# Moments first behind conv2, and most Fourier steps between conv1's chunks

## The chip, the cores and the metric

The kernel runs on one core of a Trainium2 chip. The metric is the device time of one execution in microseconds (us). The core has TensorE (PE), VectorE (DVE), ScalarE (ACT), GpSimd (POOL) and SyncE (SP, which here only issues DMAs); the engines run side by side and meet only at semaphores.

## The reference, cut to what matters

```
x = edge_filter(x)                         # prologue: 3x3 conv, softmax, weighted sum of shifts
for j in range(4):                         # 32 channels, 8 images of 64x64
    Kj, Lj = project(K[j]), project(L[j])
    z = relu(batchnorm(conv3x3(x, Kj)))    # conv1, norm 1
    x = x + 0.1 * conv3x3T(z, Kj)          # conv2
    x = batchnorm(x, gamma[j], beta[j])    # moments, norm 2, affine
    t = 1.0 / (0.1 * abs(fft2(Lj)) ** 2 + 1.0)
    x = real(ifft2(fft2(x) * t))
```

The Fourier stage is linear and acts on each channel alone, so the kernel runs it on x before norm 2 is known and applies norm 2's scale and bias to its result (the "affine" step).

## The kernel before, in words

Images go in four pairs (bp 0 to 3). A pair's convolution is four chunks, so conv1 and conv2 have 16 chunks each; a chunk is 12 matmuls into one of 8 PSUM banks (`conv`, L1025). Each layer j is one list, `layer_steps(j)`, and every engine walks that list and does its own part of each step. So a step's place in the list sets its place in five queues at once, each of which is strictly in order.

A pair's Fourier stage is this chain of steps:
- turn: DVE transposes the pair (L923) out of Z0, where POOL has put sums and differences of its halves (`mix_halves`, L474);
- fwdW: PE (L1164), then DVE moves the rows (L933);
- slot0 and fwdH: PE (L1179, L1181, L1193), then DVE multiplies by the layer's table (L957, L968);
- slot0c: PE (L1204), then ACT keeps it (L641); the inverse needs it;
- invH: PE (L1221, in the last layer L1218), then DVE moves (L939);
- invW: PE (L1236), and back: DVE transposes (L950), then POOL adds and subtracts halves (`unmix_halves`, L484);
- affine: ACT scales (L657) in two halves, and SP copies each scaled half, moved by two partition groups, from X0 to X2 (`shift_two`, L389 and L390). conv1 of the next layer reads X0 and X2, so chunks 0, 4, 8 and 12 wait for such copies (`x2_in`).

Norm 2 needs sums over all of x: ACT makes them chunk by chunk (`sum_x`, L635), DVE closes them (moments, L855 to L860), PE averages over partitions (L1139), DVE ends the norm (to L880). `prepare` (L707, four instructions) makes the weights of conv1 and of the next conv2 out of the next layer's parameters; `sum_kernels` (L697) comes ahead of it. `prepare_taps` (L719 to L731) starts the next layer's table, behind conv1's chunk 6. On DVE conv1's statistics are L810, and conv2's result is added to x by L908. ACT copies conv1's result out of PSUM (L550).

A step that takes a bank waits until the bank's last use is drained. `number_banks` gives banks in the list's order, so a new order also changes who waits for whom. fwdW and invW take four banks at once.

## Time and profile before

| | us |
|---|---|
| median of 3 runs (698.69 to 700.88) | 698.69 |
| the profiled execution | 700.2 |
| its span | 698.4 |
| PE busy in the span | 619.7 |
| DVE busy | 493.7 |
| ACT busy | 343.7 |
| POOL busy | 233.3 |

The profile is of one execution; 1.8 us of its time lie outside the span. Layers 0, 1 and 2 start conv2 at 179.73, 316.39 and 453.19 and repeat each other nearly to the 0.1 us, so what is read in one holds for three. Layer 1's conv2 runs from 316.4 to 379.5, layer 2's conv1 from 395.4 to 447.0. The last layer starts conv2 at 591.48 and has no conv1 behind it.

### The profile page before, as it was taken

The numbers are of one execution on the slowest core, as the hardware profiler recorded it, in microseconds if no ns is written. First come the engines' busy times: TensorE is split into PE (matmuls) and PEld (weight loads), VectorE is DVE, ScalarE is ACT, GpSimd is POOL, SyncE is SP. The second block draws the span as 40 slices with busy tenths as digits, with TensorE's granted clock in tenths as the row PEclk, the third lists the DMA queues.
The fourth block names the chain that finished last, engine by engine and source line by source line (L and its number), as shares of the span: only waits on it lengthen the run. The fifth ranks groups of instructions, "written<-read, shape, count | busy, mean of one in ns | idle before, by whom it ended". The sixth has DMA issues, their size and how long they took to land.

```text
span 698.4 us, 14578 instructions
## 1 busy us (share of the span) xinstructions
PE 619.7 (89%) x5840; PEld 200.9 (29%) x5840; DVE 493.7 (71%) x875; ACT 343.7 (49%) x640; POOL 233.3 (33%) x180
## 2 busy tenths in 40 slices
PE   6498999999999979999898899998978989989783
PEld 4122333222332223233232222332222223323221
DVE  2679888865786785738868767486778554867674
ACT  1466666652894322419932314299223233982232
POOL 0367666771142432202225222022252220222200
PEclk9699999999999999999999999999999999999988
DMA  9995111117600022294000224930004159000044
GB/s 187 182 168 97 32 32 33 31 31 161 157 1 1 1 63 62 70 224 116 1 2 1 70 55 107 224 79 1 2 1 109 30 133 218 3 2 1 1 123 120
DMA packets 44786, 51.21 MB, mean 73 GB/s; under 512 B 36528, under 2 KB 36656, under 8 KB 42672
## 3 DMA queue, kind: packets, MB, share of 16 engines
q1 hardware_dynamic: 40240, 48.99, 32.8%
q10 hardware_dynamic: 4480, 1.30, 1.2%
q8 instruction: 47, 0.77, 0.5%
q14 instruction: 19, 0.16, 0.1%
HBM read 11.99 MB, written 4.19 MB: 23 GB/s over the span
## 4 chain that ended last, share of the span: by engine, by line
PE 54%; ACT 20%; DVE 14%; issue 6%; DMA 3%; SPq 1%; POOL 0%; DVEq 0%; ACTq 0%; POOLq 0%
PE psum L1025 29%; ACT Z L613 10%; PE psum L1097 6%; ACT work L635 6%; PE psum L1164 3%; PE psum L1048 3%; DVE Z L950 2%; DMA X<-X 2%; PE psum L1221 2%; PE psum L1193 2%; PE psum L1236 2%; DVE work L923 2%; PE psum L1085 2%; DVE work L968 2%; DVE work L933 1%
## 5 line engine op out<-in xcount | busy, mean ns | idle before, releaser
L1025 PE MATMUL psum<-X,wts 128*32 128x512 f32 x1536 | 171.3, 594 | 9.1 <-DMA X<-X 5.0
L1025 PE MATMUL psum<-Z,wts 128*32 128x512 f32 x1536 | 172.3, 594 | 4.3 <-DVE Z L890 4.3
L474 POOL TENSOR_TENSOR Z<-X 128x512 f32<-128x512 f32 x64 | 80.8, 1286 | 251.2 <-DVE X L908 251.2
L635 ACT ACTIVATE work<-X,small 128x512 bf16<-128x512 f32 x128 | 90.7, 710 | 87.7 <-DVE X L908 87.7
L550 ACT ACTIVATE Z<-psum 128x512 f32<-128x512 f32 x64 | 38.2, 596 | 140.4 <-PE psum L1025 129.3
L484 POOL TENSOR_TENSOR X<-Z 128x1024 f32<-128x1024 f32 x24 | 56.9, 2394 | 113.0 <-DVE Z L950 113.0
L810 DVE BATCH_NORM_STATS2 stats<-Z 128x6 f32<-128x512 f32 x60 | 41.0, 691 | 69.7 <-ACT Z L550 69.6
L1025 PEld LDWEIGHTS psum<-Z,wts 128*32 128x32 f32 x1536 | 50.1, 109 | 115.5 <-issue 106.9
L613 ACT ACTIVATE Z<-Z,small 128x512 f32<-128x512 f32 (+4 forms) x92 | 80.3, 922 | 5.2 <-DVE small L880 4.7
L1025 PEld LDWEIGHTS psum<-X,wts 128*32 128x32 f32 x1536 | 47.8, 109 | 121.4 <-issue 109.8
L908 DVE SCALAR_TENSOR_TENSOR X<-psum,X 128x512 f32<-128x512 f32 x64 | 44.2, 690 | 36.2 <-PE psum L1025 36.0
L933 DVE STREAM_TRANSPOSE work<-psum 128x512 f32<-128x512 f32 x64 | 40.0, 698 | 18.3 <-PE psum L1164 18.3
L950 DVE STREAM_TRANSPOSE Z<-psum 128x512 f32<-128x512 f32 x64 | 39.9, 681 | 8.0 <-PE psum L1236 8.0
L799 DVE TENSOR_TENSOR work<-Z,psum 128x512 f32<-128x512 f32 x52 | 33.6, 680 | 16.9 <-PE psum L1085 16.9
L968 DVE TENSOR_TENSOR work<-psum,tabT 128x496 f32<-128x496 f32 x64 | 38.6, 665 | 5.8 <-PE psum L1193 5.8
L1164 PE MATMUL psum<-work,cstS 32*64 32x512 f32 x384 | 33.1, 639 | 8.9 <-DVE Z L950 4.9
L1097 PE MATMUL psum<-work,cstS 128*32 128x512 f32 x168 | 36.9, 631 | 2.9 <-DVE spare L799 2.7
L799 DVE TENSOR_TENSOR spare<-Z,psum 128x512 f32<-128x512 f32 x48 | 30.9, 679 | 4.8 <-PE psum L1085 4.6
L464 POOL TENSOR_TENSOR tabT<-Z,work 128x512 f32<-128x512 f32 x21 | 24.9, 1197 | 25.0 <-PE psum L1097 25.0
L534 ACT ACTIVATE work<-psum 128x512 f32<-128x512 f32 x53 | 30.6, 594 | 3.6 <-PE psum L1085 1.0
L923 DVE STREAM_TRANSPOSE work<-Z 128x512 f32<-128x512 f32 x48 | 31.0, 705 | 0.0
L1193 PE MATMUL psum<-work,cstS 64*64 64x496 f32 x256 | 30.3, 589 | 0.0
(127 smaller groups left out, 819.5 us busy)
## 6 DMA issues: line engine op xcount, KB each, us to landing
...
```

The source lines that it names most:

```text
L474: nc.gpsimd.tensor_tensor(rows(Z0, REG, bp, CH * (2 * half + i), CH), low, high, op=op)\
L484: nc.gpsimd.tensor_tensor(dst, even, odd, op=op).then_inc(parts_added, 1)
L613: last = nc.scalar.activation(z, z, ACT.Relu, bias=small[p0:p1, 13:14], scale=small[p0:p1, 12:13])
L635: nc.scalar.activation(by_row(rest[:, o:o + N // 2].bitcast(bf16)), xc, what, bias=small[:, 26:27], accum_out=sums[:, NCH * i + c:NCH * i ...
L799: nc.vector.tensor_tensor(by_line(product(c, dj, r)), around(c, dj, r), by_line(bank(n)), op=ALU.mult)\
L923: last = nc.vector.transpose(dst[:, b], src.rearrange("p g (e l b) -> p b g e l", e=2, b=2)[:, b])
L933: nc.vector.transpose(freqw[:, N * q:N * q + N], src).then_inc(rows_moved, 1)
L950: last = nc.vector.transpose(dst, src)
L968: nc.vector.tensor_tensor(to, src, tt, op=ALU.mult).then_inc(drained[n % BANKS], 1)
L1025: last = nc.tensor.matmul(out_b[C * r:C * r + C, :], weights[:, o:o + C], rows(src, reg, bp, g, CH, dj - 1), start=(dj == 0), stop=(dj == ...
L1097: last = nc.tensor.matmul(bank(n)[C * r:C * r + C, :], cm(C_STACK, C), product(c, dj, r), start=(dj == 0), stop=(dj == 2), tile_position=( ...
L1164: last = nc.tensor.matmul(bank(first + r)[64 * half:64 * half + 64, :], cstS[k, C_FW + 64 * hi:C_FW + 64 * hi + 64], src[:, hi], start=(hi ...
```

## The change

Layers 0 to 2, behind conv2 (the last layer has a list of its own, `last_steps`, close to the old order):
- Pair 1's invH goes ahead of conv2's chunk 14 and pair 2's fwdW behind it (before: the other way round, each one chunk earlier or later).
- slot0c of pairs 0 and 1 goes behind the next conv2 chunk. A new step, "scaled", says where DVE multiplies by the table; before, that was at the PE steps.
- Behind conv2 stand half of pair 2's fwdH, its slot0 and pair 1's invW, then moments and norm 2, and then the other half of fwdH. On DVE back of pair 1, the second half of the multiplication and turn of pair 3 stand behind the norm.
- Pair 2's slot0c and invH and pair 3's fwdW move from ahead of conv1's chunk 0 to behind chunks 0, 2 and 3. The steps after them move back too: pair 2's invW from behind chunk 2 to behind 4, pair 3's fwdH from 1 to 5, its invH from 3 to 6, its invW from 5 to 7.
- `prepare` is cut in two: conv1's half behind conv2's chunk 13, the other at its old place.
- `mix_halves` of the last chunk waits for norm 2, and ACT's sums are spread over conv2's chunks by a table, SUMS.

```diff
@@ layer_steps
-        9: fourier(j, 1, "fwdW"),
+        9: [("slot0c", j, 0)] + fourier(j, 1, "fwdW"),
-        13: fourier(j, 2, "fwdW"),
-        14: fourier(j, 1, "invH"),
-        15: fourier(j, 2, "fwdH"),
+        13: fourier(j, 1, "invH"),
+        14: fourier(j, 2, "fwdW"),
-    steps += [("moments", j), ("norm", j, 2), ("affine", j, 0), ("turn", j, BP - 1), ("weights", j)]
-    steps += fourier(j, 1, "invW") + [("back", j, 1)] + fourier(j, 3, "fwdW") + fourier(j, 2, "invH")
+    steps += quarters("fwdH", j, 2, (0, 1)) + [("slot0", j, 2), ("scaled", j, 2, 0)] + fourier(j, 1, "invW")
+    steps += [("moments", j), ("norm", j, 2)] + quarters("fwdH", j, 2, (2, 3))
+    steps += [("affine", j, 0), ("back", j, 1, 0), ("back", j, 1, 1)]
+    steps += [("scaled", j, 2, 1), ("turn", j, BP - 1), ("weights", j)]
...
+        6: [("slot0c", j, 3)] + fourier(j, 3, "invH"),
+        7: fourier(j, 3, "invW") + [("back", j, 3, 0), ("back", j, 3, 1)],
@@ mix_halves (POOL)
+                if bp == BP - 1 and i == 1 and j + 1 < DEPTH:
+                    pool.wait_ge(bn_ready, 2 * j + 2)
@@ DVE, "weights" and conv2's chunk 13
-                        prepare()
+                        prepare((1,))
...
                             sum_kernels(j + 1)
+                            prepare((0,))
@@ forward_h (PE)
+                if q == 0:
+                    pe.wait_ge(rows_moved, Q * (BP * j + c // Q + 1))
```

What this does to the queues, at three places. First DVE in layer 0, from back of pair 0 over conv2's chunks 13 to 15; before:

```order
L950 STREAM_TRANSPOSE Z<-psum 128x2x8x32 x4
L908 SCALAR_TENSOR_TENSOR X<-psum,X 128x4x128
L697 TENSOR_REDUCE ksum<-parS 128x64
L933 STREAM_TRANSPOSE work<-psum 128x512 x4
L908 SCALAR_TENSOR_TENSOR X<-psum,X 128x4x128
L939 STREAM_TRANSPOSE spare<-psum 128x8x2x32 x4
L908 SCALAR_TENSOR_TENSOR X<-psum,X 128x4x128
L957 TENSOR_TENSOR work<-psum,tabT 128x64
L968 TENSOR_TENSOR work<-psum,tabT 128x16x31 x4
L855 TENSOR_REDUCE small<-sums 128x2
```

and the same place now (in this file L968 is back, L926 conv2's sum, L725 `prepare`, L957 and L951 the moves of invH and fwdW, L986 the multiplication, L873 the first of moments):

```order
L968 STREAM_TRANSPOSE Z<-psum 128x2x8x32 x4
L926 SCALAR_TENSOR_TENSOR X<-psum,X 128x4x128
L715 TENSOR_REDUCE ksum<-parS 128x64
L725 SCALAR_TENSOR_TENSOR wts<-ksum,cstS,parS 128x96 x2
L957 STREAM_TRANSPOSE spare<-psum 128x8x2x32 x4
L926 SCALAR_TENSOR_TENSOR X<-psum,X 128x4x128
L951 STREAM_TRANSPOSE work<-psum 128x512 x4
L926 SCALAR_TENSOR_TENSOR X<-psum,X 128x4x128
L986 TENSOR_TENSOR work<-psum,tabT 128x16x31 x2
L975 TENSOR_TENSOR work<-psum,tabT 128x64
L873 TENSOR_REDUCE small<-sums 128x2
```

Two of the weights' instructions now stand between chunk 13's sum and the moves, and two multiplications instead of four ahead of the moments. Second PE in layer 0, from conv2's chunk 15 to conv1's first chunks; before:

```order
L1025 MATMUL psum<-Z,wts 32x512 x12
L1179 MATMUL psum<-work,cstS 128x2x16
L1181 MATMUL psum<-work,cstS 64x2x16 x2
L1193 MATMUL psum<-work,cstS 64x496 x8
L1204 MATMUL psum<-work,cstS 64x2x16 x4
L1139 MATMUL psum<-small,cstS 128x5
L1236 MATMUL psum<-spare,cstS 32x512 x16
L1164 MATMUL psum<-work,cstS 64x512 x16
L1221 MATMUL psum<-work,cstS 64x512 x8
L1025 MATMUL psum<-X,wts 32x512 x24
```

and now (L1047 is a convolution, L1219 fwdH, L1262 invW, L1161 the average, L1230 slot0c, L1247 invH, L1188 fwdW):

```order
L1047 MATMUL psum<-Z,wts 32x512 x12
L1219 MATMUL psum<-work,cstS 64x496 x4
L1203 MATMUL psum<-work,cstS 128x2x16
L1205 MATMUL psum<-work,cstS 64x2x16 x2
L1262 MATMUL psum<-spare,cstS 32x512 x16
L1161 MATMUL psum<-small,cstS 128x5
L1219 MATMUL psum<-work,cstS 64x496 x4
L1047 MATMUL psum<-X,wts 32x512 x12
L1230 MATMUL psum<-work,cstS 64x2x16 x4
L1047 MATMUL psum<-X,wts 32x512 x24
L1247 MATMUL psum<-work,cstS 64x512 x8
L1047 MATMUL psum<-X,wts 32x512 x12
```

invW now stands ahead of the average, and nothing but half of fwdH stands between the average and conv1. Third DVE in layer 0 behind conv1's chunk 4; before:

```order
L810 BN_STATS stats<-Z 128x6 x2
L950 STREAM_TRANSPOSE Z<-psum 128x2x8x32 x4
L810 BN_STATS stats<-Z 128x6
L719 TENSOR_REDUCE lsum<-parS 128x32
L721 SCALAR_TENSOR_TENSOR lsum<-lsum,parS 128x96
L724 TENSOR_SCALAR lsum<-lsum,cstS 128x32
L725 SCALAR_TENSOR_TENSOR lsum<-lsum,cstS 128x32
L728 TENSOR_TENSOR work<-lsum,cstS 128x1024
L731 TENSOR_TENSOR work<-work,lsum 128x1024
L810 BN_STATS stats<-Z 128x6 x8
```

and now (L828 is the statistics, L737 to L749 `prepare_taps`, L957 invH's move, L968 back):

```order
L828 BN_STATS stats<-Z 128x6
L737 TENSOR_REDUCE lsum<-parS 128x32
L739 SCALAR_TENSOR_TENSOR lsum<-lsum,parS 128x96
L742 TENSOR_SCALAR lsum<-lsum,cstS 128x32
L743 SCALAR_TENSOR_TENSOR lsum<-lsum,cstS 128x32
L746 TENSOR_TENSOR work<-lsum,cstS 128x1024
L749 TENSOR_TENSOR work<-work,lsum 128x1024
L957 STREAM_TRANSPOSE spare<-psum 128x8x2x32 x4
L828 BN_STATS stats<-Z 128x6
L968 STREAM_TRANSPOSE Z<-psum 128x2x8x32 x4
L828 BN_STATS stats<-Z 128x6 x7
```

`prepare_taps` kept its place behind chunk 6, and pair 3's invH move and back, which stood ahead of it, now stand behind it.

## Rows read from the trace of the kernel before

**Rows 1.** Page, part 5: ACT's copies, count, busy us and mean ns, idle.
```profile
L550 ACT ACTIVATE Z<-psum 128x512 f32<-128x512 f32 x64 | 38.2, 596 | 140.4 <-PE psum L1025 129.3
```

**Rows 2.** Timeline: start us, us, engine, instruction [idle before <-releaser]; layer 1's conv2.
```profile
336.47 5.36 PE L1025 MATMUL psum<-Z,wts 128*32 128x512 f32 x48
...
349.88 0.66 PE L1164 MATMUL psum<-third,cstS 32*64 32x512 f32 x4 [1.50 <-ACT work L641]
...
370.29 0.66 PE L1164 MATMUL psum<-work,cstS 32*64 32x512 f32 x4 [1.22 <-DVE Z L950]
```

**Rows 3.** Timeline, DVE and POOL behind conv2's chunk 13 in layer 1.
```profile
370.11 4.74 POOL L484 TENSOR_TENSOR X<-Z 128x1024 f32<-128x1024 f32 x2 [7.58 <-DVE Z L950]
...
370.53 1.19 DVE L697 TENSOR_REDUCE ksum<-parS 128x64 f32<-128x576 f32 x1
...
376.03 2.51 DVE L939 STREAM_TRANSPOSE spare<-psum 128x512 f32<-128x512 f32 x4 [0.29 <-PE psum L1221]
...
379.63 0.69 DVE L908 SCALAR_TENSOR_TENSOR X<-psum,X 128x512 f32<-128x512 f32 x1 [1.09 <-PE psum L1025]
```

**Rows 4.** Timeline from moments to conv1's first chunk, layer 1.
```profile
383.51 0.18 DVE L855 TENSOR_REDUCE small<-sums 128x2 f32<-128x32 f32 x1
...
384.75 0.36 PE L1139 MATMUL psum<-small,cstS 128*128 128x5 f32 x2 [2.58 <-DVE small L860]
...
385.19 3.61 PE L1236 MATMUL psum<-spare,cstS 64*32 64x512 f32 x32
...
387.15 2.38 ACT L657 ACTIVATE X<-X,small 128x1024 f32<-128x1024 f32 x2 [1.23 <-DVE small L880]
...
389.39 0.97 DVE L707 SCALAR_TENSOR_TENSOR wts<-ksum,cstS,parS 128x96 f32<-128x96 f32 x4
...
389.53 1.98 PE L1164 MATMUL psum<-work,cstS 32*64 32x512 f32 x32 [0.73 <-DVE work L923]
...
395.39 5.36 PE L1025 MATMUL psum<-X,wts 128*32 128x512 f32 x48 [1.35 <-DVE work L933]
...
410.60 1.95 PE L1221 MATMUL psum<-work,cstS 64*64 64x512 f32 x16
```

**Rows 5.** Windows: stretch, us, PE, PEld, DVE, ACT, POOL busy, PEclk, DMA, GB/s.
```profile
386.00:387.00 1.00, 1.00 (x24) 0.38 (x16) 0.86 (x6) 0.00 (x0) 0.00 (x0) 0.50 0.00 0
...
665.00:672.00 7.00, 5.13 (x49) 1.10 (x34) 5.39 (x11) 4.81 (x4) 0.00 (x0) 0.51 0.41 105
```

**Rows 6.** Timeline, DVE in the prologue, beside POOL and without it.
```profile
58.56 2.00 DVE L707 SCALAR_TENSOR_TENSOR wts<-ksum,cstS,parS 128x96 f32<-128x96 f32 x4
...
58.80 1.19 POOL L464 TENSOR_TENSOR X<-Z,work 128x512 f32<-128x512 f32 x1
...
58.88 1.23 DVE L707 SCALAR_TENSOR_TENSOR wts<-ksum,cstS,parS 128x96 f32<-128x96 f32 x1
...
159.82 0.24 DVE L724 TENSOR_SCALAR lsum<-lsum,cstS 128x32 f32<-128x32 f32 x1
```

**Rows 7.** Timeline, conv1's second half in layer 1; last row layer 2.
```profile
419.64 15.67 PE L1025 MATMUL psum<-X,wts 128*32 128x512 f32 x144
...
422.46 4.77 POOL L484 TENSOR_TENSOR X<-Z 128x1024 f32<-128x1024 f32 x2 [7.02 <-DVE Z L950]
...
423.13 0.69 DVE L810 BATCH_NORM_STATS2 stats<-Z 128x6 f32<-128x512 f32 x1 [0.74 <-ACT Z L550]
...
425.02 2.26 DVE L724 TENSOR_SCALAR lsum<-lsum,cstS 128x32 f32<-128x32 f32 x1
...
428.74 1.23 DVE L731 TENSOR_TENSOR work<-work,lsum 128x1024 f32<-128x1024 f32 x1
...
430.71 2.36 ACT L657 ACTIVATE X<-X,small 128x1024 f32<-128x1024 f32 x2
...
436.52 10.51 PE L1025 MATMUL psum<-X,wts 128*32 128x512 f32 x96 [1.22 <-DMA X<-X]
...
574.82 10.51 PE L1025 MATMUL psum<-X,wts 128*32 128x512 f32 x96 [2.67 <-DMA X<-X]
```

More of the change, by code:

```diff
@@ L156, in layer_steps, with last_steps @@
     for c in range(NCH):
[L157 to L160 removed]
+        steps += [("conv1", j + 1, c)] + rest.get(c, [])
+    return steps
+def last_steps(j):
+    steps = fourier(j, 2, "fwdH") + [("slot0c", j, 2), ("moments", j), ("norm", j, 2), ("affine", j, 0), ("turn", j, BP - 1)]
+    steps += fourier(j, 1, "invW") + [("back", j, 1, 0), ("back", j, 1, 1)] + fourier(j, 3, "fwdW") + fourier(j, 2, "invH")
+    steps += [("affine", j, 1)] + fourier(j, 3, "fwdH") + [("slot0c", j, 3)] + fourier(j, 2, "invW")
+    steps += [("back", j, 2, 0), ("back", j, 2, 1)] + fourier(j, 3, "invH") + fourier(j, 3, "invW")
+    return steps + [("back", j, 3, 0), ("back", j, 3, 1), ("affine", j, 2), ("affine", j, 3)]
+SUMS = {c: (c,) for c in range(5)} | {6: (5,), 8: (6,), 9: (7,), 10: (8,), 11: (9, 10), 12: (11,), 13: (12, 13), 14: (14,), 15: (15,)}
 ORDER = prologue_order()
```

53 lines of the change are left out of this document (29 added, 24 removed).

## The prediction, made before the change was run

> **What bounds the kernel now.** I read first the busy times by engine, then the timeline of PE with the idle time ahead of each group, then, at each pause, what released it. PE is busy for 619.7 of 698.4 us and the others far less, so time can come only from PE's pauses, from work at a low clock, or go into new pauses. In layer 1's conv2 PE pauses for ACT and DVE, 1.50 us at most [rows 2]. Behind conv2 the large pause stands: 2.58 us ahead of the average, then invW at 3.61 us, which takes 1.95 elsewhere, and short pauses up to conv1 at 395.39 [rows 4]. In that stretch the granted clock is 0.50, 1.2 instead of 2.4 GHz [rows 5]. So such a drop costs 3.61 - 1.95 = 1.66 us. Behind that PE runs nearly without a pause to chunk 12, which waits 1.22 us for the copy of the last scaled image [rows 7]. Layers 0, 1 and 2 are alike, so a layer's sum counts three times.
>
> I walk through layer 1 with its own times: conv chunk 2.7 us, 2.6 in a run (15.67 for six) [rows 7]; fwdW, invH, invW 1.9 each [rows 4]; fwdH 1.7, slot0 0.6, slot0c 0.3; a DVE move of four 2.5 [rows 3]; an ACT copy 0.6 [rows 1].
>
> **conv2, part by part.** Up to chunk 8 nothing moves; it ends at 341.8. slot0 and fwdH end at 344.1, chunk 9 at 346.8, and slot0c no longer waits. fwdW of pair 1 needs chunk 9 added by DVE, 348.15, where it started at 349.88 before [rows 2]. ACT's sums are not late for it, since SUMS leaves one out. Chunk 11 ends at 357.4, fwdH at 359.7, chunk 12 at 362.4; invW of pair 0 waits until chunk 12 is drained, 363.4, and chunk 13 ends at 368.0 against 369.0 before. Back ends at 368.1, and POOL starts unmix at once, for 4.74 us [rows 3], so to 372.9. DVE adds chunk 13 (to 368.8), sums the kernels (1.19, to 370.0) and comes to the two new instructions of `prepare` in the middle of unmix.
>
> Here is the **price of the cut `prepare`**. Alone, four take 0.97 us [rows 4]. Beside POOL they took 2.00: the first ended with one POOL instruction, and the second lasted 1.23, to the end of the next, which began at 58.80 [rows 6]. L724 shows the same: 0.24 without POOL [rows 6], 2.26 beside unmix, to unmix's end [rows 7]. Unmix is two instructions of about 2.37, so the first of the two gets through at 370.5 and the second at 372.9: DVE goes on at 373.1 and not at 370.5. The bounds are 0.5 us (both get through between POOL's two) and 3.1; I take 3.1, by the nearest row, the second L707. Behind DVE stands invH's move (373.1 to 375.6), and fwdW of pair 2 needs three quarters of it, so PE, which has ended chunk 14 at 372.6, pauses 2.5 us to 375.1. Chunk 15 ends at 379.7 and is added at 379.9, where it was 379.63 [rows 3]. So of 2.2 us that the new order wins in conv2, nothing is left. And a pause of 2.5 us is next to the one of 2.58: I take the drop of the clock for it too, **+1.66**; its bounds are 0 and 1.66.
>
> **From conv2 to conv1.** Before, from chunk 15's addition to affine 387.15 - 379.63 = 7.52 us. Now DVE multiplies only two quarters and slot0 ahead of moments, but fwdH starts later, behind the row moves; moments start 2.6 us behind the addition and not 3.9, so affine follows it by 6.3. PE's invW (1.9) fits in ahead of the average. From affine to conv1 before 8.24, since conv1 waited for DVE's move of fwdW's rows. Now it waits for the copy alone: from ACT's start to a conv1 chunk released by the copy 436.52 - 430.71 = 5.8 [rows 7]. So conv1 starts at 379.9 + 6.3 + 5.8 = 391.9 and not at 395.39: **-3.5**. But PE has ended the second half of fwdH at about 385.5 and stands still for some 6 us, longer than the pause in rows 4, so the first chunks of conv1 run at the low clock: **+1.65** (bounds 0.8 and 2.6, since rows 5 show a stretch of 7 us at 0.51).
>
> **Moved into conv1.** What filled the wait before has its price now: slot0c 0.3, invH 1.9, fwdW 1.9: **+4.1**. The copy for chunk 4 is asked for behind chunk 2's copy on ACT, and PE does invH, chunk 3 and fwdW meanwhile, 6.5 us against 0.6 + 5.8: no margin, no price. invW of pair 2 waits for the moves of fwdW, which DVE starts 2.3 us behind fwdW's start: **+0.3**.
>
> **Behind chunk 6** three queues meet. ACT's affine 2 waits for POOL's unmix, whose last half ends about when chunk 6 does; then 1.24 for the second half, 0.6 for chunk 6's copy, slot0c's copy 0.3, and invH of pair 3 needs that: 1.9 us of pause. DVE: statistics 0.7 behind the copy, then `prepare_taps`, which takes from the end of chunk 6's statistics at 423.8 to 430.0, 6.2 us [rows 7], of which 2.0 are L724's wait for POOL; unmix is over by then, so 4.2; then invH's move, 2.5. invW of pair 3 needs that. From chunk 6's end 0.1 + 1.75 + 0.7 + 4.2 + 2.5 + 0.1 = 9.3 us. PE has slot0c, invH and chunk 7 in that time, 4.9: **+4.4**. Behind it back, unmix and affine 3 lie as before, and affine 3 still stands behind chunk 9's copy, so chunk 12's wait stays.
>
> **The sum.** A layer: -3.5 + 1.66 + 1.65 + 4.1 + 0.3 + 4.4 = +8.6; three layers +25.8. The last layer has no `prepare` and no unmix; it keeps the win in conv2, about 2.0 of the 2.2, and its tail is in the old order: -2.0. Together +23.8, so the profiled execution's 700.2 would be 724.0. Its own time is 1.5 above the median; on the median the sum gives 698.69 + 23.8 = 722.5.
>
> **A rule weighed.** Rows 4 and 5 show that a pause of 2.58 us was followed by the low clock, all four times. The Trainium skill, page "TensorE: Matmul & The Clock Gate", section "Why this matters for your kernels", warns only of pauses longer than this one. By it the pause ahead of fwdW costs nothing but itself, and the sum is 5.0 lower.
>
> **Rivals.**
> - No drop for the 2.5 us pause: 25.8 - 5.0 - 2.0, 717.5. For it: the pause of 1.50 us led to none [rows 2]; against it, the four of 2.58. The skill's rule above speaks for it.
> - The two `prepare` instructions slip between POOL's two: then the conv2 win stays, per layer -2.6 of stall and no drop ahead of fwdW, 8.6 - 4.3 = 4.3; 698.69 + 13.0 - 2.0 = 709.7. Against it: both rows of rows 6.
> - More drops: invW of pair 3 waits some 2.5 us as well, and the low stretch at conv1's start can be the long one. +1.66 and +0.9 a layer: 730.
> - Faster: the pauses behind chunk 6 are covered. That needs ACT, DVE's taps and the move to fit in the 4.9 us that PE has from chunk 6 to invW 3, and `prepare` not to stall. Then -6.1 (the early start without the stall) + 4.1 + 0.3 + 1.65 = 0.0 a layer, and with the -2.0 of the last layer 696.6; with no drop at conv1's start 691.7. It decides at 4.9 us: 4.2 + 2.5 alone are more, so it needs DVE to do these steps in another order than its queue has.
> - The change starts conv1 early only on paper: the copy lands later than 5.8, as in layer 2, where chunk 12 waited 2.67 and not 1.22 [rows 7]. +1.45 a layer, 726.9.
>
> **Chances.** Forecast with all its terms (719 to 726) 0.35; no drop for the short pause 0.2; `prepare` slipping through, with or without parts of the rest (705 to 715), 0.17; more drops or late copies (over 726) 0.17; the faster rival 0.07; little changed 0.04. The range 706 to 730 leaves out the faster rival, the unchanged case and the end of the slow ones. Three tenths of a per cent, 2 us, is what a measurement of this kernel can tell from no change: faster 0.07, within 0.05, slower 0.88.
>
> **What would show it.** Behind conv2's chunk 13 one of two DVE weight instructions lasting over 2 us and a PE pause of about 2.5 us ahead of fwdW; conv1 starting about 3.5 us (2 with the drop) earlier relative to conv2's start than now, out of a PE pause of 6 us, with PEclk at 0.5 there; pauses of about 1.9 and 2.5 us ahead of pair 3's invH and invW, the latter released by the move; chunk 12 still waiting about 1.2 us; conv2 starts 8.6 us further apart than the 136.8 us of now. I would be wrong above all if DVE got through beside unmix, or if `prepare_taps` took well under 4.2 us.

## The result, and the profile after

The changed kernel takes 723.04 us (median of 4 runs, 718.95 to 724.63), the kernel before 699.4 (4 runs on the same chip, 698.69 to 700.88): a ratio of 1.033, with a 95% interval of 1.028 to 1.037. Slower, as forecast; the prediction was 722.5 in a range of 706 to 730. The profiled run took 723.0, its span is 721.1.

The page of after, the head and part 1, the granted clock of part 2, and the groups of part 5 that changed:

```profile
span 721.1 us, 14584 instructions
...
PE 627.7 (87%) x5840; PEld 200.6 (28%) x5840; DVE 498.1 (69%) x875; ACT 344.0 (48%) x640; POOL 233.0 (32%) x180
...
PEclk9699999999999879999999899999998999999988
...
L1047 PE MATMUL psum<-X,wts 128*32 128x512 f32 x1536 | 180.3, 615 | 25.2 <-issue 20.3
L1047 PE MATMUL psum<-Z,wts 128*32 128x512 f32 x1536 | 172.4, 594 | 4.3 <-DVE Z L908 4.3
```

PE's instructions are the same 5840. Its busy time is 8.0 us more (619.7 before) and its idle time 14.7 us more. Of the 8.0 some 5 are low clock (an estimate: what the slow groups of both timelines take over their usual length); the rest I put down to the moved steps, which break conv1's chunks into shorter runs. Conv1's convolutions take 180.3 us against 172.4 for conv2's, which have the same count and shapes, and the idle time ahead of them is 25.2 us, 20.3 of it ahead of chunk 0.

To see where the time went I cut each layer at three starts in PE's timeline: stretch A from conv2's chunk 0 to conv1's chunk 0, B from there to conv1's chunk 12, C from there to the next conv2. The last layer has no conv1 and is one stretch, up to the end of the span. All in us:

| kernel | A, layers 0, 1, 2 | B, layers 0, 1, 2 | C, layers 0, 1, 2 | last layer | from conv2 of layer 0 to the end |
|---|---|---|---|---|---|
| before | 79.0, 79.0, 79.0 | 41.0, 41.1, 42.6 | 16.7, 16.7, 16.7 | 106.9 | 518.7 |
| after | 77.1, 75.4, 75.4 | 54.3, 51.3, 52.8 | 16.7, 16.7, 18.4 | 105.0 | 542.9 |
| difference | -1.9, -3.6, -3.6 | +13.3, +10.2, +10.2 | 0, 0, +1.7 | -1.9 | +24.2 |
| forecast | -1.8 each | +10.5 each | 0 | -2.0 | +23.8 |

What lies ahead of layer 0's conv2 is the same work in both, and takes 178.1 to 183.8 us over the kernels of this study without a pattern; so I compare the last column, and give the medians beside it. That column is of one execution each, and the runs of the kernel before alone, over all chips, lie between 697.6 and 706.4 us: differences of a few us in it say little by themselves, and the stretches in which they arise say more.

After's PE timeline in layer 1, where conv2 starts 9.83 us later than before's (columns as in [rows 2]):

```profile
326.22 18.25 PE L1047 MATMUL psum<-Z,wts 128*32 128x512 f32 x168 [1.07 <-DVE Z L908]
...
385.04 0.66 PE L1188 MATMUL psum<-work,cstS 32*64 32x512 f32 x4 [2.28 <-DVE spare L957]
...
393.51 0.36 PE L1161 MATMUL psum<-small,cstS 128*128 128x5 f32 x2
...
401.60 4.05 PE L1047 MATMUL psum<-X,wts 128*32 128x512 f32 x24 [6.75 <-issue]
...
432.48 1.95 PE L1247 MATMUL psum<-work,cstS 64*64 64x512 f32 x16 [1.41 <-ACT work L658]
...
439.36 1.09 PE L1262 MATMUL psum<-spare,cstS 64*32 64x512 f32 x16 [2.22 <-DVE spare L957]
...
452.88 10.51 PE L1047 MATMUL psum<-X,wts 128*32 128x512 f32 x96 [1.12 <-DMA X<-X]
```

The pause of 2.58 us ahead of the average [rows 4] is gone. A pause of 2.28 us ahead of fwdW has come, one of 6.75 ahead of conv1's chunk 0, with 4.05 us for a chunk of 2.78 behind it, and pauses of 1.41 and 2.22 ahead of pair 3's invH and invW. Chunk 12 waits 1.12 us, where it was 1.22 [rows 7]. DVE and POOL where the pause ahead of fwdW comes from, to be read against [rows 3]:

```profile
378.19 4.76 POOL L501 TENSOR_TENSOR X<-Z 128x1024 f32<-128x1024 f32 x2 [7.54 <-DVE Z L968]
...
380.07 2.99 DVE L725 SCALAR_TENSOR_TENSOR wts<-ksum,cstS,parS 128x96 f32<-128x96 f32 x2
382.99 2.50 DVE L957 STREAM_TRANSPOSE spare<-psum 128x512 f32<-128x512 f32 x4
```

Two small instructions of `prepare` take 2.99 us and end when POOL's unmix does. In the code they wait for no semaphore of POOL, so that the engines meet only at semaphores, as the description of the chip says above, does not hold for DVE and POOL here. Behind chunk 6 ACT and DVE show where the other two pauses come from:

```profile
428.08 1.25 ACT L674 ACTIVATE X<-X,small 128x1024 f32<-128x1024 f32 x1 [1.83 <-POOL X L501]
430.44 1.24 ACT L674 ACTIVATE X<-X,small 128x1024 f32<-128x1024 f32 x1 [1.11 <-POOL X L501]
...
432.07 0.27 ACT L658 ACTIVATE work<-psum 128x64 f32<-128x64 f32 x1
...
432.81 0.43 DVE L737 TENSOR_REDUCE lsum<-parS 128x32 f32<-128x288 f32 x1
...
433.57 0.24 DVE L742 TENSOR_SCALAR lsum<-lsum,cstS 128x32 f32<-128x32 f32 x1
...
436.54 2.51 DVE L957 STREAM_TRANSPOSE spare<-psum 128x512 f32<-128x512 f32 x4
```

ACT waits for each half of unmix (1.83, 1.11), and only then copies the chunk and slot0c. DVE's tap weights run from 432.81 to 436.5, and the move for invW stands behind them.

### The profile page after: what moved, and what is told of

It is laid out like the page before. It is cut to its first block, busy times and chain, and to the rows that moved or that the text cites. A ratio compares the mean times of both kernels' runs of the same rounds, so it can differ in the third digit from the quotient of the medians.

```text
span 721.1 us, 14584 instructions
## 1 busy us (share of the span) xinstructions
PE 627.7 (87%) x5840; PEld 200.6 (28%) x5840; DVE 498.1 (69%) x875; ACT 344.0 (48%) x640; POOL 233.0 (32%) x180
## 4 chain that ended last, share of the span: by engine, by line
PE 56%; DVE 18%; issue 14%; POOL 5%; ACT 3%; DMA 3%; SPq 1%; DVEq 0%; ACTq 0%; POOLq 0%
PE psum L1047 31%; PE psum L1119 6%; PE psum L1188 4%; POOL X L501 4%; PE psum L1262 3%; DMA X<-X 2%; PE psum L1070 2%; DVE spare L957 2%; DVE work L986 2%; DVE work L951 2%; PE psum L1107 2%; PE psum L1219 2%; DVE X L926 1%; DVE wts L725 1%; ACT X L674 1%
## 5 line engine op out<-in xcount | busy, mean ns | idle before, releaser
L1047 PE MATMUL psum<-X,wts 128*32 128x512 f32 x1536 | 180.3, 615 | 25.2 <-issue 20.3
L1047 PE MATMUL psum<-Z,wts 128*32 128x512 f32 x1536 | 172.4, 594 | 4.3 <-DVE Z L908 4.3
L652 ACT ACTIVATE work<-X,small 128x512 bf16<-128x512 f32 x128 | 90.7, 710 | 76.7 <-DVE X L926 76.3
L828 DVE BATCH_NORM_STATS2 stats<-Z 128x6 f32<-128x512 f32 x60 | 41.4, 690 | 89.0 <-ACT Z L567 89.0
L1047 PEld LDWEIGHTS psum<-X,wts 128*32 128x32 f32 x1536 | 47.2, 112 | 146.2 <-issue 133.9
L1047 PEld LDWEIGHTS psum<-Z,wts 128*32 128x32 f32 x1536 | 50.3, 109 | 121.9 <-issue 113.7
L630 ACT ACTIVATE Z<-Z,small 128x512 f32<-128x512 f32 (+4 forms) x92 | 80.3, 922 | 5.2 <-DVE small L898 4.7
L926 DVE SCALAR_TENSOR_TENSOR X<-psum,X 128x512 f32<-128x512 f32 x64 | 43.5, 680 | 29.0 <-PE psum L1047 28.4
L951 DVE STREAM_TRANSPOSE work<-psum 128x512 f32<-128x512 f32 x64 | 39.9, 685 | 20.6 <-PE psum L1188 20.6
L968 DVE STREAM_TRANSPOSE Z<-psum 128x512 f32<-128x512 f32 x64 | 40.1, 684 | 14.3 <-PE psum L1262 14.2
L986 DVE TENSOR_TENSOR work<-psum,tabT 128x496 f32<-128x496 f32 x64 | 38.8, 664 | 5.5 <-PE psum L1219 5.2
L1188 PE MATMUL psum<-work,cstS 32*64 32x512 f32 x384 | 34.6, 656 | 8.2 <-DVE spare L957 6.8
L674 ACT ACTIVATE X<-X,small 128x1024 f32<-128x1024 f32 x24 | 29.1, 1237 | 13.6 <-POOL X L501 9.8
L1219 PE MATMUL psum<-work,cstS 64*64 64x496 f32 x256 | 31.0, 591 | 0.5 <-DVE work L951 0.2
```

Source lines behind the costliest of these rows:

```text
L630: last = nc.scalar.activation(z, z, ACT.Relu, bias=small[p0:p1, 13:14], scale=small[p0:p1, 12:13])
L652: nc.scalar.activation(by_row(rest[:, o:o + N // 2].bitcast(bf16)), xc, what, bias=small[:, 26:27], accum_out=sums[:, NCH * i + c:NCH * i ...
L926: nc.vector.scalar_tensor_tensor(xc, in0=by_row(bank(n)), scalar=STEP, in1=xc, op0=ALU.mult, op1=ALU.add).then_inc(drained[n % BANKS], 1)
L951: nc.vector.transpose(freqw[:, N * q:N * q + N], src).then_inc(rows_moved, 1)
L986: nc.vector.tensor_tensor(to, src, tt, op=ALU.mult).then_inc(drained[n % BANKS], 1)
L1047: last = nc.tensor.matmul(out_b[C * r:C * r + C, :], weights[:, o:o + C], rows(src, reg, bp, g, CH, dj - 1), start=(dj == 0), stop=(dj == ...
```

## The experiments

The theory is the sum of the prediction: two stalls on DVE (`prepare` beside POOL, the tap weights ahead of the move), one on ACT (affine 2 ahead of slot0c), a pause of PE ahead of conv1 with a low clock behind it, and 4.1 us of work moved into conv1. The main rival from the result: the low clock, and not the stalls, is what costs, and comes back somewhere else when a stall is taken out. Three runs of the changed kernel take out one of these each; two more take out several. The others try the change's order inside conv2 without the rest, what the low clock costs, and what delays a copy. The table has all of them, in the columns of the table above; the ratios are those to the kernel before of the same chip, with their 95% intervals:

| kernel | A | B | C | last layer | to the end | median, ratio |
|---|---|---|---|---|---|---|
| `prepare` behind chunk 12 | 73.0, 73.1, 73.0 | 51.2, 54.0, 55.4 | 16.7, 16.7, 18.4 | 103.3 | 534.7 | 718.11, 1.022 (1.016 to 1.027) |
| taps behind chunk 8 | 75.4, 75.4, 75.4 | 50.4, 49.4, 51.7 | 16.7 each | 103.6 | 531.3 | 714.09, 1.016 (1.012 to 1.020) |
| PE kept busy | 76.9, 75.3, 75.3 | 51.6, 51.6, 51.5 | 16.7 each | 103.3 | 535.6 | 716.96, 1.021 (1.017 to 1.025) |
| both cures | 73.0, 73.1, 73.1 | 50.1, 50.1, 51.6 | 16.7 each | 103.6 | 524.5 | 707.61, 1.011 (1.007 to 1.016) |
| no stalls | 73.1, 73.0, 73.0 | 46.8, 46.8, 46.8 | 16.7 each | 105.8 | 515.3 | 696.27, 0.994 (0.991 to 0.997) |
| new conv2 alone | 78.0, 77.3, 77.2 | 41.0, 41.1, 42.4 | 16.7 each | 103.4 | 510.4 | 694.94, 0.988 (0.983 to 0.993) |
| banks | 76.5, 76.7, 77.2 | 41.0, 40.9, 43.2 | 16.7, 16.7, 18.1 | 103.6 | 510.5 | 692.00, 0.987 (0.983 to 0.991) |
| invW first | 80.0, 79.6, 79.9 | 41.3, 40.9, 43.7 | 16.7, 16.7, 18.0 | 103.6 | 520.3 | 700.53, 1.001 (0.998 to 1.003) |
| before, kept busy | 79.8, 79.8, 80.3 | 41.0, 41.0, 41.0 | 16.7 each | 106.1 | 519.0 | 700.28, 0.999 (0.996 to 1.001) |
| banks, kept busy | 78.4, 78.4, 78.5 | 41.5, 41.5, 41.4 | 16.7 each | 105.8 | 515.4 | 696.29, 0.993 (0.990 to 0.996) |
| new conv2, shifted | 77.9, 77.3, 77.2 | 41.0, 41.0, 41.0 | 16.7 each | 105.0 | 510.4 | 693.33, 0.989 (0.984 to 0.993) |
| banks, shifted | 77.0, 76.6, 77.3 | 42.0, 41.0, 41.7 | 16.7 each | 103.4 | 509.0 | 688.41, 0.982 (0.977 to 0.986) |

**`prepare` behind chunk 12**, where POOL has nothing to do:

```diff
-                        elif at[1] == 13 and j + 1 < DEPTH:
+                        elif at[1] == 12 and j + 1 < DEPTH:
                             sum_kernels(j + 1)
                             prepare((0,))
```

> The changed kernel with the sum of the kernels and conv1's half of prepare one chunk earlier, behind conv2's chunk 12, where POOL stands still until back is done. My theory (the two weight instructions wait for POOL's unmix): the second one takes 0.25 us instead of about 2.8, the pause of 2.27 us ahead of pair 2's fwdW goes, conv1 starts some 2.5 us earlier after conv2's start in layers 0 to 2, total 7 to 10 us below the changed kernel (the upper end if drops of the clock go with it). Rival (the pause ahead of fwdW is the move of invH, wherever prepare stands, or the time is given back in front of moments): within 2 us of the changed kernel.

Its timeline in layer 1: DVE's `prepare` and the first fwdW of pair 2 on PE, then conv1's chunk 0 and pair 3's invW.

```profile
368.85 0.55 DVE L725 SCALAR_TENSOR_TENSOR wts<-ksum,cstS,parS 128x96 f32<-128x96 f32 x2
...
377.21 0.66 PE L1188 MATMUL psum<-work,cstS 32*64 32x512 f32 x4
...
393.81 5.31 PE L1047 MATMUL psum<-X,wts 128*32 128x512 f32 x24 [6.77 <-issue]
...
432.82 3.50 PE L1262 MATMUL psum<-spare,cstS 64*32 64x512 f32 x32 [2.22 <-DVE spare L957]
```

The two instructions take 0.55 us and fwdW has no pause. Stretch A is 73.0 us in all three layers, 2.35 less than after's layers 1 and 2, and 4.0 less than layer 0, which had the low clock there too. So the stall was worth 2.35 us a layer. (The edit also moves the sum of the kernels, 1.2 us, out of the way; but the two instructions alone became 2.44 us shorter, more than the pause.) In all, 8.2 us less than the changed kernel, within the 7 to 10 expected. B is longer by 2.7 and 2.6 us in layers 1 and 2 for another reason: chunk 0 takes 5.31 and not 4.05, and invW of pair 3 3.50 and not 1.95. On that point the rival is right: the low clock came in other places, and took part of the gain.

**The taps behind chunk 8**, where PE has a run of chunks ahead of it that needs nothing from DVE:

```diff
-                        if at[1] == 6:
+                        if at[1] == 8:
```

> The changed kernel with prepare_taps behind conv1's chunk 8 instead of 6, so behind pair 3's invH move and back on DVE, and now beside POOL's unmix of pair 3. My theory: the pause of 2.2 us ahead of pair 3's invW goes; that of 1.4 us ahead of invH stays, since it is ACT's; total 6 to 9 us below the changed kernel. Rival (chunk 12 waits for affine 3 anyway, so what is won there is waited for later): chunk 12's wait grows from 1.1 to 3.3 us and the total stays within 2 us.

PE at the same place in layer 1, pair 3's invH, chunk 7 and invW, and DVE's L742 of the moved taps:

```profile
431.19 1.95 PE L1247 MATMUL psum<-work,cstS 64*64 64x512 f32 x16 [1.42 <-ACT work L658]
...
435.78 1.95 PE L1262 MATMUL psum<-spare,cstS 64*32 64x512 f32 x32
...
443.02 2.26 DVE L742 TENSOR_SCALAR lsum<-lsum,cstS 128x32 f32<-128x32 f32 x1
```

invW follows chunk 7 at once. L742, beside POOL's unmix again, takes 2.26 us and not 0.24, and nobody waits for it. So the same instruction is long beside unmix and short without it, as those of `prepare` are. Chunk 12 waits no longer than before in layers 0 and 1 (1.01 and 1.10), so the rival is out. The gain is 11.6 us, more than the 6 to 9 expected: 6.7 are the pause (2.23 in each layer); most of the rest is where the low clock fell: not at fwdW in layer 0 (A -1.7), not at invW in layer 0 (-1.3), not in layer 2's C (-1.7) and not in the last layer (-1.4), but more at chunk 0 in layers 1 and 2 (+0.4, +1.3).

**PE kept busy ahead of conv1**: six matmuls ahead of each of the three conv1, into the bank that chunk 0 overwrites.

```diff
+                if c == 0 and j:
+                    bk.claim(NUMBER["conv1", j, c])
+                    for _ in range(6):
+                        nc.tensor.matmul(bank(NUMBER["conv1", j, c]), cm(C_AVG), cstS[:, 0:N], start=True, stop=True)
```

> The changed kernel with six matmuls of 128 by 512 added in PE's 6.8 us pause ahead of conv1's chunk 0 in layers 1 to 3, into the bank that chunk 0 then overwrites; they are beside the computation. My theory (conv1's start pays for a low clock): PEclk stays 1.00, chunk 0 takes 2.8 us instead of 4.05 and 5.35, total 4 to 7 us below the changed kernel. Rival (chunk 0 is slow from the copies that land beside it, or the clock falls all the same): chunk 0 keeps over 4 us, total within 2 us or higher.

PE's timeline in layer 1, the added matmuls (each in two records), conv1's chunk 0, and pair 3's invW:

```profile
395.97 5.42 PE L1060 MATMUL psum<-cstS 128*128 128x512 f32 x12
402.75 2.78 PE L1047 MATMUL psum<-X,wts 128*32 128x512 f32 x24 [1.36 <-DMA X<-X]
...
439.23 3.49 PE L1266 MATMUL psum<-spare,cstS 64*32 64x512 f32 x32 [2.22 <-DVE spare L957]
```

The pause of 6.75 becomes 5.42 us of work and one of 1.36, released by the copy; chunk 0 takes 2.78 in all three layers and starts when it did. So the low clock behind the long pause cost 1.3 to 2.6 us a layer, as much as chunk 0 was over 2.78, 5.1 in all. In all three layers invW of pair 3 now ran slow, 3.24 to 3.61 us behind a pause of 2.22, where after had it in one: 3.2 of the 5.1 us went there. Most of the total gain of 7.3 us (4 to 7 expected) is therefore not the theory's: layer 2's chunk 12 waited 0.99 us and not 2.60 and ran at full clock behind it, 3.3 us together, and the last layer, which the edit doesn't touch, was 1.7 shorter.

**Both cures together:**

> The changed kernel with both cures at once: the first half of prepare behind conv2's chunk 12 instead of 13, and the tap weights behind conv1's chunk 8 instead of 6. Alone, from conv2's start in layer 0 to the end of the span, the first took 8.2 us off the changed kernel's 542.9 and the second 11.6. If the two stalls are what they seem, two pauses far apart with nothing shared, the gains add: 542.9 - 19.8 = 523.1 from conv2's start on, and about 1.006 times the kernel before (518.7 + 4.4). The rival: part of each gain was the low clock, and this comes back at another pause when one is removed (invW of pair 3 ran at 3.5 us in two layers of the first cure). Then the second cure, which removes that very pause, should bring more than its own share, 521 or less; and if instead the drops are only moved on to conv1's start and chunk 12, less than the sum, 526 or more.

524.5 us from conv2's start, 1.4 over the sum of the two, and between the two numbers by which the expectation would know the rival. A has the first one's 73.0 and B the second one's lack of a pause. The stalls are apart, and their gains add, as near as the low clock lets one see: chunk 0 of conv1 takes 5.2 to 5.4 us in all three layers, in after 4.1 in two of them.

**No stalls**: both cures, the matmuls ahead of conv1, and ACT's affine 2 behind chunk 6's slot0c:

```diff
-        5: fourier(j, 3, "fwdH") + [("affine", j, 2)],
-        6: [("slot0c", j, 3)] + fourier(j, 3, "invH"),
+        5: fourier(j, 3, "fwdH"),
+        6: [("slot0c", j, 3), ("affine", j, 2)] + fourier(j, 3, "invH"),
```

> Both cures, and on top: affine of quarter 2 stands behind chunk 6's slot0c instead of behind chunk 5, so ACT's slot0c copy does not queue behind it (pause of 1.41 us ahead of invH of pair 3), and six 128x512 matmuls whose result is overwritten run in the pause ahead of conv1's chunk 0 in layers 1 and 2 and the first. By my sum what is then left of the change is the moved work (+4.1 a layer), conv1 started earlier by 3.5 + 2.6 = 6.1, invW of pair 2 +0.3, and no low clock at conv1's start: -1.7 a layer, and -2.0 in the last layer: 518.7 - 5.1 - 2.0 = 511.6 from conv2's start on, ratio about 0.99. The rival, that the moved work costs more than its own busy time in conv1 (copies for chunks 4 and 12 come late, affine 2 now delays its own chunk), gives 518 to 521 and a ratio of 1.00 or over.

PE's timeline in layer 1: conv1's chunk 0, invW of pair 2, invH of pair 3:

```profile
387.64 2.78 PE L1047 MATMUL psum<-X,wts 128*32 128x512 f32 x24 [1.36 <-DMA X<-X]
...
405.69 1.95 PE L1266 MATMUL psum<-work,cstS 64*32 64x512 f32 x32 [0.42 <-DVE work L951]
...
416.46 1.95 PE L1251 MATMUL psum<-work,cstS 64*64 64x512 f32 x16 [0.63 <-ACT work L658]
```

All three layers are alike to 0.1 us. A is 6.0 us shorter than before's, where the sum had 6.1. B is 5.7 longer than before's layer 1: 4.2 are the moved work (slot0c 0.35, invH 1.9, fwdW 1.9), 0.42 and 0.63 are pauses ahead of invW and invH, and the rest, 0.5, I take for the gaps between more and shorter runs of chunks, since a chunk that stands alone takes 2.7 us and one in a run 2.6. So without its stalls the change is worth -0.1 and -0.3 us in layers 0 and 1, and not my -1.7, because pauses and gaps around the moved work cost 1.5 where I had 0.3. In layer 2 it is -1.8, since before's chunk 12 waits 1.6 us longer there, which is no merit of the order (see "Shifted"). The last layer has 105.8, 0.8 more than after's, with invW and fwdW at the low clock. My expectation was 3.7 too low, and the rival's 2.7 too high.

**The new conv2 alone**: the change's order inside conv2, and all that stands behind it as before.

```diff
-    steps += quarters("fwdH", j, 2, (0, 1)) + [("slot0", j, 2), ("scaled", j, 2, 0)] + fourier(j, 1, "invW")
-    steps += [("moments", j), ("norm", j, 2)] + quarters("fwdH", j, 2, (2, 3))
-    steps += [("affine", j, 0), ("back", j, 1, 0), ("back", j, 1, 1)]
+    steps += fourier(j, 2, "fwdH") + [("slot0c", j, 2), ("moments", j), ("norm", j, 2), ("affine", j, 0)]
...
-                        prepare((1,))
+                        prepare((0, 1))
...
-                            prepare((0,))
```

> One part of the change alone: the new order inside conv2 (slot0c one chunk later, pair 1's invH ahead of pair 2's fwdW, the spread sums), and behind conv2 the old order, with all of prepare at its old place and no wait on POOL. My theory: 2.0 to 2.2 us less in each of four layers, since the new order is only spoilt by prepare's stall: 690 to 692 us, faster than the kernel before by over 1%. Rival (the order in conv2 is worth something only in the last layer, where no unmix and no sum of kernels stand on DVE): 696 to 699 us.

510.4 us, 8.3 less than before: A -1.0, -1.7 and -1.8, and -3.5 in the last layer, where fwdW takes 1.98 us and in before 3.72. The expectation had 2.0 to 2.2 in each of four layers: its total (8.0 to 8.8) came by luck, since the three layers gave less and the clock in the last one made up for it. This part of the change is good for about 1.2% (0.988, against the kernel before on the same chip), and the rest of it, with its `prepare` and its steps in conv1, costs 32.5 us on top.

One more thing stands in its timeline of layer 1, from the average to conv1:

```profile
386.73 1.95 PE L1254 MATMUL psum<-spare,cstS 64*32 64x512 f32 x32 [0.24 <-issue]
...
388.54 2.38 ACT L669 ACTIVATE X<-X,small 128x1024 f32<-128x1024 f32 x2 [1.23 <-DVE small L893]
...
390.92 2.98 PE L1180 MATMUL psum<-work,cstS 32*64 32x512 f32 x32 [2.23 <-DVE work L936]
...
394.16 2.50 DVE L946 STREAM_TRANSPOSE work<-psum 128x512 f32<-128x512 f32 x4
...
396.80 5.36 PE L1041 MATMUL psum<-X,wts 128*32 128x512 f32 x48 [0.39 <-DVE work L946]
```

Here invW ran at 1.95 us behind a pause of 2.57 and not at 3.61 [rows 4], and yet conv1 starts 396.80 - 388.54 = 8.26 us behind affine, where it was 8.24. The prediction had taken 1.66 us as what such a drop costs. (fwdW ran slow here in its place, 2.98 us, so this row alone doesn't settle it.)

**Before, kept busy** asks for that directly:

```diff
+                for _ in range(4 if which == 2 else 0):
+                    nc.tensor.matmul(bank(n), cm(C_AVG), cstS[:, 0:N], start=True, stop=True)
                 pe.wait_ge(moments_in, 2 * j + which)
```

> The kernel before with one addition: ahead of the average behind conv2 PE runs four 128x512 fp32 matmuls whose result is overwritten, so that its pause of 2.58 us becomes one of under 1 us. It asks what the low clock behind that pause costs, 3.61 us for invW instead of 1.95, which the prediction took as 1.66 us. First theory, from the two runs just taken: in the run with the new conv2 alone, layer 1 ran this invW at 1.95 us, and yet conv1 started 8.26 us behind affine, where the kernel before needs 8.24; DVE runs without a gap from the average to its move of the rows that conv1's bank waits for, so PE's slow invW costs nothing there. invW then takes 1.95 in all layers, conv1 starts as before, and the time stays within 2 us of the kernel before, ratio 1.00. The rival: the drop costs 1.66 in each of four layers and the time falls by 5 to 7 us, ratio 0.991.

PE's timeline in layer 1: the four matmuls, the average, invW, fwdW, conv1:

```profile
383.21 3.70 PE L1139 MATMUL psum<-cstS 128*128 128x512 f32 x8
386.75 0.28 PE L1141 MATMUL psum<-small,cstS 128*128 128x5 f32 x2
386.96 1.95 PE L1238 MATMUL psum<-spare,cstS 64*32 64x512 f32 x32
391.45 2.47 PE L1166 MATMUL psum<-work,cstS 32*64 32x512 f32 x32 [2.54 <-DVE work L923]
...
397.31 4.93 PE L1025 MATMUL psum<-X,wts 128*32 128x512 f32 x44 [0.36 <-DVE work L933]
```

The four took 3.70 us, more than the pause, so the average comes 0.9 us later than before (386.75 - 317.50 against 384.75 - 316.39), and conv1 0.8 later. invW takes 1.95 in all four layers. If its slow run had cost 1.66 us, conv1 would have started 0.8 earlier; it didn't, and not in layer 0 either (A 79.8), where fwdW took 1.98 as well. So in layers 0 to 2 the drop there costs next to nothing: PE waits for DVE behind it, 2.54 us now where it was 0.73. The 1.66 us are what invW loses, not what the kernel loses. The total says less than A does, since it hides two other things: chunk 12 of layer 2 waits 1.07 us and not 2.67, and the last layer is 0.8 us shorter although its average comes 0.9 later. There fwdW took 1.98 us and not 3.72, so in the last layer, which has no conv1, the low clock did cost.

**Banks**: the kernel with the new conv2, with invH of pair 2 ahead of fwdW of pair 3, and with conv1's half of `prepare` behind conv2's chunk 12. (The expectation speaks of chunks 12 and 14; in the kernel that ran the other half of `prepare` stays at its old place, behind the norm.)

```diff
-    ... + fourier(j, 3, "fwdW") + fourier(j, 2, "invH")
+    ... + fourier(j, 2, "invH") + fourier(j, 3, "fwdW")
...
-                        prepare((0, 1))
+                        prepare((1,))
...
-                        elif at[1] == 13 and j + 1 < DEPTH:
+                        elif at[1] == 12 and j + 1 < DEPTH:
                             sum_kernels(j + 1)
+                            prepare((0,))
```

> The kernel before's order behind conv2 with the changed kernel's order inside conv2 (as in the run with the new conv2 alone, which took 510.4 us from conv2's start on), and two more edits: invH of pair 2 ahead of fwdW of pair 3, so that the bank that conv1's chunk 0 takes is not the one whose rows DVE has to move last, and prepare split over chunks 12 and 14 of conv2. The first says that the wait before conv1 (1.35 us in the kernel before, released by DVE) is a matter of the bank and not of the copy: conv1 then starts 1.3 us earlier in each of three layers, and the split brings up to 0.5 more: 505 to 506 us, ratio about 0.98. The rival: the copy of the first scaled image lands no earlier than that, and the pause only changes its releaser: 509 to 511.

In the total 510.5 us, as with conv2 alone. A is 1.5 and 0.6 us shorter than with conv2 alone in layers 0 and 1, and the same in layer 2. The pause only changed its place: chunk 0 follows fwdW at once, and fwdW waits 1.85 to 3.62 us for DVE's move of back. PE's timeline, fwdW and conv1 in layer 1, and fwdW in layer 2:

```profile
390.86 1.98 PE L1183 MATMUL psum<-work,cstS 32*64 32x512 f32 x32 [2.43 <-DVE Z L963]
392.77 5.36 PE L1042 MATMUL psum<-X,wts 128*32 128x512 f32 x48
...
524.91 2.71 PE L1183 MATMUL psum<-work,cstS 32*64 32x512 f32 x32 [3.62 <-DVE Z L963]
```

The rival holds for the total (510.5), though not its reason. The releaser is DVE's back (L963), and not the copy; fwdW's own input was turned 3.2 us before it starts, so I read the wait as one for the banks that back frees, late in DVE's queue.

**invW first**, ahead of the moments:

```diff
-    steps += fourier(j, 2, "fwdH") + [("slot0c", j, 2), ("moments", j), ("norm", j, 2), ("affine", j, 0)]
+    steps += fourier(j, 2, "fwdH") + [("slot0c", j, 2)] + fourier(j, 1, "invW") + [("moments", j), ("norm", j, 2), ("affine", j, 0)]
...
-    steps += fourier(j, 1, "invW") + [("back", j, 1, 0), ("back", j, 1, 1)] + ...
+    steps += [("back", j, 1, 0), ("back", j, 1, 1)] + ...
```

> As the run on banks, with invW of pair 1 taken out from behind the turn and put behind slot0c, ahead of the average, where PE pauses for 2.58 us in the kernel before and then runs invW at 3.61 us instead of 1.95. If filling the pause keeps the clock up, PE saves invW's extra 1.66 us and starts conv1 up to that much earlier: 500 to 502 us from conv2's start on, ratio 0.97. The rival: DVE, not PE, sets the pace there (its moments stand behind the row moves, and conv1 waits for the copy), so that PE only waits longer ahead of conv1, and the pause there, longer now, puts the clock down at conv1's chunk 0: no gain against the run on banks, or 1 us a layer lost.

PE's timeline in layer 1: invW of pair 1, the second half of invH, fwdW:

```profile
384.06 1.95 PE L1257 MATMUL psum<-spare,cstS 64*32 64x512 f32 x32 [0.58 <-issue]
...
392.60 1.99 PE L1242 MATMUL psum<-work,cstS 64*64 64x512 f32 x8 [5.17 <-issue]
395.64 3.42 PE L1183 MATMUL psum<-work,cstS 32*64 32x512 f32 x32 [1.05 <-DVE work L952]
```

The pause of 2.58 is filled, and one of 5.17 stands in the middle of invH. 520.3 us, 9.8 more than banks and worse than the rival expected. invH's second half starts while DVE's move of back runs; I read that as the bank which this move frees, which wasn't tested. fwdW behind it takes 3.42 us and conv1 needs it.

**Banks, kept busy**, with the four 128x512 matmuls ahead of the average:

> The run on banks (510.5 us from conv2's start in layer 0 to the end of the span) with the same four matmuls ahead of the average. In that run layers 0 and 1 took 134.1 and 134.3 us, 1.2 less than with the new conv2 alone, but layer 2 took 138.6: fwdW at 2.71 us behind a pause of 3.62, chunk 12 to 15 at 11.98 instead of 10.51 behind a pause of 2.44. Theory: DVE sets the pace from the average to conv1, and the drops behind other pauses fall where they will, so these matmuls change little: invW at 1.95, layers between 134 and 138, 508 to 512. The rival: PE kept busy there holds the clock up for all that comes behind it up to conv1, fwdW takes 1.98 in every layer, and layer 2 comes to 136 or less: 505 to 507.

515.4 us, more than either theory had. The matmuls delay the average by 0.9 us, as in before, and fwdW, now behind a pause of 3.78 us, takes 3.11 to 3.17 us in each of the three layers, where banks had 1.98, 1.98 and 2.71. Here work ahead of one pause did not keep the clock up behind the next.

**Shifted.** Layer 2's chunk 12 waits 2.67 us in before and 1.22 in layer 1 [rows 7]. I looked for what else moves in that copy. Queues of the DMA engines in half a microsecond of before, 571.0 to 571.5, and in the run below, 565.0 to 565.5:

```profile
q8 instruction: 1, 0.02, 14.3%
```

```profile
q8 instruction: 1, 0.02, 10.9%
```

SyncE's issues and PE's chunk 12 of before, layer 2:

```profile
568.81 0.46 SPq L389 DMA_DIRECT2D X<-X  x1
...
574.82 1.50 PE L1025 MATMUL psum<-X,wts 128*32 128x512 f32 x12 [2.67 <-DMA X<-X]
```

One packet of the queue named `instruction`, 0.02 MB, moves while the copy is under way (issued from 568.81 on). Before and after and the twelve experiments have 42 such copies ahead of a chunk 12. In eight of them, all in layer 2, this packet starts 3.0 to 3.4 us ahead of chunk 12, and the wait is 2.4 to 2.8 us; in the other 34 it starts 4.3 us or more ahead, and the wait is 0.9 to 1.2. (The expectation below has these distances by half microseconds and a little too large.) Four matmuls of 128x8 in the pause ahead of the average shift the place of that packet:

```diff
+                for _ in range(4 if which == 2 else 0):
+                    nc.tensor.matmul(bank(n)[:, 0:8], cm(C_AVG), cstS[:, 0:8], start=True, stop=True)
```

> The run with the new conv2 alone, plus four very small fp32 matmuls of 128x8 ahead of the average in PE's pause there, whose result is overwritten: they cost no time that anyone waits for, but shift where in the program each load of instructions falls. It asks why chunk 12 of conv1 waits 2.4 to 2.7 us for its copy in layer 2 of eight kernels (this one: 2.46) and about 1.0 in layers 0 and 1. In each of these eight an instruction packet of 0.02 MB moves 3.3 to 3.6 us ahead of chunk 12, while the copy runs; in the kernels with added matmuls it moves 6.5 us or more ahead, and the wait is 1.0 to 1.1. Theory: the packet delays the copy. With the shift it falls ahead of the copy in layer 2, the wait is 1.1 there, and that layer is 1.4 us shorter than 136.3: 509 from conv2's start on, instead of 510.4. The rival: the wait belongs to layer 2 for another reason (the copy's own address or the 6 us of kept clock in those kernels), then it stays at 2.4 to 2.7. If the packet lands in the copy of another layer, that layer should show the long wait instead.

The same two rows of its timeline, layer 2:

```profile
566.95 0.46 SPq L401 DMA_DIRECT2D X<-X  x1
...
571.38 10.51 PE L1041 MATMUL psum<-X,wts 128*32 128x512 f32 x96 [1.09 <-DMA X<-X]
```

The packet now moves at 565.0, ahead of the copy's issue, and chunk 12 starts 4.4 us behind the first issue, with a wait of 1.09; with the new conv2 alone these are 5.8 and 2.46. SyncE issues the four parts at the same distances in both, so it is the copy that is later and not its issue. Layer 2 is 134.9 us and not 136.3, as expected. The total stays at 510.4, since the last layer ran fwdW at 3.31 us here and at 1.98 there.

The same four in the kernel with the banks:

> The run on banks with the same four small matmuls. Layer 2 took 138.6 us there, with a wait of 2.44 ahead of chunk 12 and the four chunks behind it at 11.98 instead of 10.51. Theory: with the instruction packet out of the copy the wait is 1.1 and, the pause being short, the clock stays up behind it, so that layer 2 comes to about 135.5 and the whole to 507.5 from conv2's start on, the fastest of all kernels here, ratio 0.983. The rival as in the run beside it: the wait stays, 510 or more.

509.0 us, 1.5 less than banks and not 3.0: layer 2 is 135.7 as expected, but in layer 0 fwdW and conv1's first chunks ran slow (B 42.0). With 688.41 us it has the lowest median of the study, at a ratio of 0.982 (0.977 to 0.986); that of banks (0.983 to 0.991) and that of the new conv2 alone overlap it. It beats both the kernel before and the changed one.

## Why the prediction was right

The total came out right, 542.9 - 518.7 = +24.2 against +23.8, and so did the way: the stalls, the early start of conv1, the pause ahead of it and the price of the moved work are there, each near its forecast. Two terms were mis-sized, the low clock behind the short pause and the pauses behind chunk 6, and low clock that I had left out makes up for them. That part is luck.

- **The stall of `prepare`** was 2.99 us for two instructions (3.1 taken), fwdW's pause 2.28 (2.5 forecast), and removing it alone gave 2.35 us a layer. This is shown by the run.
- **The low clock behind that pause**, +1.66 a layer, is the mis-sized term. It came in layer 0 alone (A 77.1 against 75.4). Over the three kernels that have this pause, of 2.26 to 2.28 us, it came in two of nine layers, each time layer 0 (the other with PE kept busy, A 76.9). I took a pause of 2.5 for one of 2.58, all four of which had led to the drop in before [rows 4, 5]; over all runs invW was slow behind a pause of 2.57 or 2.58 us ahead of the average in 17 of 19 layers. That price, in turn, was one that before doesn't pay in layers 0 to 2: with PE kept busy there nothing was gained. In after's layer 0 it was paid, since chunk 15 and all behind it wait for PE.
- **conv1's start.** 401.60, which less the shift of 9.83 is 391.8; forecast 391.9. Its parts fit too: the last addition at 380.0 (379.9 forecast), affine 6.1 us behind it (6.3), conv1 5.7 behind affine (5.8). It starts out of a pause of 6.75 us (6 forecast), with chunk 0 at 4.05 to 5.35 us and not 2.78. Two windows of layer 1 (columns as in [rows 5]) have the granted clock: 0.50, which is 1.2 GHz, in the first 2 us, and 0.70 on average in the next 2, in which it rises:

```profile
401.00:403.00 2.00, 1.40 (x8) 0.45 (x12) 2.00 (x3) 0.00 (x0) 2.00 (x1) 0.50 0.82 194
403.00:405.00 2.00, 2.00 (x16) 0.54 (x12) 0.56 (x3) 0.00 (x0) 0.14 (x1) 0.70 0.00 0
```

- **The low clock at conv1's start** was +1.65 (bounds 0.8 and 2.6) and measured 1.27, 1.29 and 2.57. Keeping PE busy removed it at chunk 0 in all three layers, though most of it came back at pair 3's invW.
- **Moved work**: +4.1 forecast, 4.2 by its instructions, and some 0.5 more in gaps between shorter runs. invW of pair 2 waits 0.42 (0.3).
- **Behind chunk 6**: +4.4 forecast, 1.41 + 2.22 = 3.6 measured. ACT's queue cost 1.4 and not 1.9. The tap weights took 3.7 us and not 4.2: without POOL beside them not only L742 was short but also the instruction before it, 0.26 us and in before 0.77. The causes were the right ones, since moving the taps alone removed the 2.2 and left the 1.4.
- **What I had not counted** is the low clock in two more places: invW of pair 3 in layer 0 (3.22 us, +1.3) and chunks 12 to 15 in layer 2 (C, +1.7). (In the last layer fwdW is slow in both kernels, 3.61 and 3.72 us.) These 3.0 us stand against the two layers in which fwdW's drop stayed away, 3.3. The rival "more drops" named the first of them. So the total is right to 0.4 us partly by chance; the layers, +11.4, +6.5 and +8.2 against +8.6 each, show how far the clock alone moves it.
- **The last layer**: -1.9 against -2.0.
- **The rule weighed**, of the Trainium skill's "TensorE: Matmul & The Clock Gate", "Why this matters for your kernels": pauses of 2.2 to 2.6 us, shorter than those it warns of, were followed by the low clock in some layers and not in others. The sum by it was 5.0 lower than mine; the measured term was 3.3 lower than mine. The same pause of 2.22 us ahead of invW of pair 3 led to it in one layer of three in after, two with `prepare` moved and three with PE kept busy ahead of conv1; the rule's length of a pause doesn't decide here, and neither does mine.
- The rivals: "`prepare` slips through" is out (2.99 us), "faster" is out as it stands, and even with all stalls removed the change is worth 0.6% and not 1%, and of those 3.4 us 1.6 are layer 2's shorter wait for the copy; "late copies" is out for conv1's start and for chunk 12 of layers 0 and 1.

What stays open: what decides whether a pause of 2.2 to 2.6 us is followed by the low clock. It differed between layers of one run with the same pause and the same work ahead of it. Open too is by what way a packet of instructions delays a copy.
